# Edge messages of a four-layer graph network: moving one scaled part per pair of tiles from ScalarE and TensorE to VectorE

## What is computed

```python
w = ssp(edge_attr @ W_f1) @ W_f2 * (ssp(s0 @ W_s1) @ W_s2)
w1, w2, w3, w4 = jnp.split(w, 4, axis=-1)
x0e, x1e = split_irreps(x[edge_src])
sh0, sh1 = (edge_sh[:, 0], edge_sh[:, 1:4])
out0 = w1 * x0e * sh0[:, None] + w4 * (jnp.einsum('eum,em->eu', x1e, sh1) / jnp.sqrt(3.0))
out1 = w2[:, :, None] * x0e[:, :, None] * sh1[:, None, :] + w3[:, :, None] * x1e * sh0[:, None, None]
edge_feat = merge_irreps(out0, out1)
out = jax.ops.segment_sum(edge_feat, edge_dst, num_segments=old_x.shape[0])
```

## Time and profile before

| | |
|---|---|
| median of 3 runs | 1556.94 us (1551.32 to 1558.68) |
| the profiled execution | 1552.31 us, with a span of 1550.4 us |
| busy share of the span | PE 89%, DVE 74%, ACT 50%, POOL 47% |
| `interaction_edges` within the span | its steady steps lie between about 900 and 1360 us |
| granted TensorE clock there | 1.00 of full speed |

### The profile page before, as it was taken

The page is one execution under the profiler, slowest core; times in us unless marked ns, Lnnn a source line. Parts: engine busy times, 40 slices in busy tenths (PEclk is TensorE's granted clock), DMA queues, the critical chain, the costliest instruction groups (busy, mean ns, idle before and its releaser), DMA issues. The chain is left out here.

```text
span 1550.4 us, 22449 instructions
## 1 busy us (share of the span) xinstructions
PE 1379.4 (89%) x6771; PEld 820.1 (53%) x6771; DVE 1145.0 (74%) x2024; ACT 779.7 (50%) x1997; POOL 733.9 (47%) x768
## 2 busy tenths in 40 slices
PE   5589899899997939999957599999999999985998
PEld 3245577644444539989855344444444444443443
DVE  8977588641206578999936599999999999996023
ACT  2155355300000238979734188878787878761100
POOL 0000399537750357100004588888888888840000
PEclk9889999999998858979878799999999999997999
DMA  8994000000001020500011544444444444401001
GB/s 234 51 113 153 1 2 2 1 8 16 15 11 40 8 113 16 81 1 1 1 37 41 186 140 143 153 152 144 144 150 154 143 147 146 150 25 36 26 14 41
DMA packets 96964, 117.81 MB, mean 76 GB/s; under 512 B 50065, under 2 KB 78225, under 8 KB 96849
## 3 DMA queue, kind: packets, MB, share of 16 engines
q1 hardware_dynamic: 80497, 44.83, 16.5%
q0 software_dynamic: 16352, 71.55, 14.9%
HBM read 96.02 MB, written 11.55 MB: 69 GB/s over the span
## 5 line engine op out<-in xcount | busy, mean ns | idle before, releaser
L431 POOL TENSOR_SCALAR hot_i<-iota_row,il 128x128 f32<-128x128 bf16 x125 | 108.1, 881 | 178.8 <-DVE il L453 172.0
L1426 POOL DMA_INDIRECT far<-far_rows,far_node x150 | 167.6, 1118 | 43.9 <-issue 26.6
L613 POOL DMA_INDIRECT records<-recs,place_i x136 | 137.1, 1008 | 87.4 <-issue 40.9
L1041 PE MATMUL sum_ps<-wx,prob_t 128*128 128x65 f32 x1024 | 140.2, 297 | 12.2 <-DVE prob_t L1073 12.2
L1041 PEld LDWEIGHTS sum_ps<-wx,prob_t 128*128 128x128 f32 x1024 | 138.2, 217 | 13.9 <-DVE prob_t L1073 13.9
L1574 ACT ACTIVATE far<-far,recs 128x128 f32<-128x128 f32 x450 | 138.6, 386 | 0.0
L367 PE MATMUL perm_ps<-hot_high,hot_low 128*128 128x400 f32 x272 | 97.3, 521 | 21.4 <-ACT hot_high L237 21.4
L708 PE MATMUL gcn_ps<-pair,hs 128*128 128x512 f32 x256 | 112.0, 600 | 3.2 <-DVE hs L771 3.2
L1471 PE MATMUL near_ps<-near_parts,hot_t 128*128 x450 | 89.0, 335 | 10.4 <-DVE hot_t L1603 10.4
L1563 ACT ACTIVATE pair<-f_ps,recs 128x256 f32<-128x256 f32 x150 | 72.0, 480 | 51.7 <-PE s_ps L1507 51.7
L777 DVE SCALAR_TENSOR_TENSOR h<-gcn_out_ps,root_p,bias_gcn 128x512 f32<-128x512 f32 x16 | 12.0, 752 | 116.0 <-PE gcn_out_ps L718 116.0
(11 more groups left out here) (332 smaller groups left out, 3272.8 us busy)
## 6 DMA issues: line engine op xcount, KB each, us to landing
pair<-zeros SPq DMA_DIRECT2D x1, 8576.0 KB, 58.5
places<-local_rows SPq DMA_DIRECT2D x75, 64.0 KB, 3.9
s_all<-s_rows SPq DMA_DIRECT2D x8, 512.0 KB, 7.8
records<-empty_record SPq DMA_DIRECT2D x1, 2925.0 KB, 70.7
far<-far_rows,far_node POOLq DMA_INDIRECT x150, 4.7
recs<-in_edge_attr SPq DMA_DIRECT2D x1, 2176.0 KB, 26.8
records<-recs,place_i POOLq DMA_INDIRECT x136, 2.2
w_gcn<-in_L_gnn_W_gcn SPq DMA_DIRECT2D x2, 1024.0 KB, 7.4
```

Of the source, the lines that this page charges most:

```text
L431: nc.gpsimd.tensor_scalar(hot_i[:, g % 2, k, 1, :], c.iota_row[:], il[:, t + k:t + k + 1], None, ALU.is_equal).then_inc(hot_i_ready, 1)
L613: c.nc.gpsimd.indirect_dma_start(c.rows[:, :], bass.IndirectOffsetOnAxis(ap=c.place_i[:, t:t + 1], axis=0), c.recs[:, t, :], None).then_in ...
L1041: last = nc.tensor.matmul(sum_ps[b % 2][:, h // 4, at:at + DH + 1], prob_t[:, n % PS, k, :], wx[:, k, h, :], start=(k == 0), stop=(k == NB ...
L1426: nc.gpsimd.indirect_dma_start(far[:, u % UNROLL, k, :], None, c.far[:, :], bass.IndirectOffsetOnAxis(ap=far_node[:, t:t + 1], axis=0)) \
```

## The change

The table `BY_ACT` says which vector parts ScalarE makes, for the first and for the second tile of a group. For the first tile it held parts 0 and 1, and now holds part 0 alone, as for the second tile. `BY_DVE` is what is left over.

```diff
-    BY_ACT = ((0, 1), (0,))
+    BY_ACT = ((0,), (0,))
     BY_DVE = tuple(tuple(m for m in range(3) if m not in taken) for taken in BY_ACT)
```

## The result

The changed kernel is slower. Its median is 1568.99 us (1567.19 to 1572.66, 4 runs), against 1555.80 us (4 runs) before. The ratio is 1.0097, with a 95% interval of 1.0074 to 1.0121. The prediction said 1561, between 1553 and 1577, and put its highest chance (0.60) on no change that can be measured. The time is inside the range, 8 us above the value, and in the class with 0.30. Between the medians before and after lie 13.2 us, where the prediction added up 4.3.

The account below looks back on a forecast made before the run. TensorE was taken as the bound at 6.72 us, the VectorE and GpSimd loop second at 6.51, rising to 6.775. The terms 3.6 + 0.3 + 0.8 - 0.4 gave +4.3 us, so 1561 us, range 1553 to 1577.

Parts of the forecast that it names:

- What bounds the kernel now: Steady steps: TensorE's own work sets the 6.72 us period; the loop of VectorE and GpSimd is second at 6.51.
- TensorE's 0.22 and ScalarE's instruction are lost: L1518 gets 0.22 us shorter and ScalarE drops about 0.33 us; neither shortens the period, as TensorE will wait.
- The loop takes over: Closed loop through VectorE and GpSimd goes from 6.51 to 6.775 us and sets the period; forecast, chance 0.70.
- its price is the distance of starts: VectorE's fourth L1663 costs the distance between pass starts, 0.263 us, not its duration.
- The forecast's own band: Whole kernel: 1559 to 1564 us from pass price, slack and ends; 1555 to 1568 with the scatter of the runs.
- a rival in which the slack of 0.21 is not free: GpSimd's wait for L1525 costs 0.21 anyway, so the whole 0.26 shows: 1577 us; chance 0.22 together with the port rival.
- The class "slower": Measurably slower whole kernel: chance 0.30, being 0.22 from the two slower rivals plus 0.08 from scatter.
- The other price: Fourth pass on VectorE by the skill page's latency rule: 0.194 us, loop 6.70, sum about -1 us.
- The slack of 0.21: Loop of VectorE and GpSimd has 0.21 to 0.22 us to spare per step before GpSimd's L1455.
- The rival at the port: VectorE's fourth pass pushes L1667 into GpSimd's copy L1434 at the shared port: 1580 us; chance 0.22 with the slack rival.
- The sum with 0.263: Whole kernel with the pass at 0.263 us: period 6.775, +4.3 us in all, +0.3%.
- The longer path at 6.62: Two-period path from L1625 through TensorE, L1525, L1455 and L1650 to a later L1625: 6.62 us a period, not binding.

Follow-up runs that it names:

- e2: Kernel before with only TensorE's half of the change: L1518 has 256 columns instead of 384, one term left out; 1540.65 us.
- e8: Changed kernel with one more VectorE pass per group ahead of L1650, written to an unread slot; 1569.67 us, period 6.908.
- e1: Kernel before with only VectorE's half of the change: one more fused pass per group, written to an unread slot; 1568.18 us, period 6.908.
- e11: Changed kernel with GpSimd's copy L1434 ahead of its two gathers; the period falls by 0.048 us.
- e9: Changed kernel with L1667 between the third and the fourth fused pass; 1561.48 us, ratio 1.0035.
- e10: Kernel of e9 with one L1611 moved behind L1603 as well; 1550.02 us, ratio 0.9976.
- e12: Kernel of e10 with L1518 at 128 columns instead of 256, one term left out; 1548.33 us, ratio 0.9963.
- e7: Changed kernel with only the second of the two L1611 moved behind L1603; ratio 1.0003, period 6.711.
- e3: Changed kernel with both L1611 moved behind L1603; 1576.42 us.
- e5: Changed kernel with a fifth fused VectorE pass; ScalarE keeps part 0 of the first tile only, L1523 has 128 columns; 1588.82 us.
- e6: Changed kernel with L1667 ahead of the four fused passes; 1587.16 us.
- e4: Kernel before with both L1611 moved behind L1603; slower by 1%, steps of 6.79 and 7.12 us alternate.

## Why the prediction was right or wrong

*What bounds the kernel now: right.* TensorE's own work set 6.72, and the loop of L1455, L1650, the passes, L1603 and L1444 stood at 6.51. e2 runs at 6.519 with nothing but 128 columns of L1518 taken away. VectorE's 49.7 of 50 us was no bound: e8 puts 0.26 us more into its queue at no cost.

*TensorE's 0.22 and ScalarE's instruction are lost: right.* e1 has neither and runs at the changed kernel's period.

*The loop takes over, at 6.51 plus the price of a pass: right. The price: wrong.* The step that failed is the term "its price is the distance of starts", 0.263. The fourth pass costs 0.363 at the place where it lands, and the first L1611 0.04 more, so the loop is 6.908 and not 6.775. Over 69 steady steps that is 9.2 us, and it accounts for the 8.9 between the forecast's rise of 4.3 and the 13.2 measured. The rest of the sum held about: for the first step and the last ones 1.1 us were forecast, and the trace has 0.4 in the first and 0.7 in the last four. The prediction also named a growing row of L1663 among the signs that it is wrong. That row grew, from 0.34 to 0.44 us.

*The range: right by its allowance.* The forecast's own band ended at 1564, and at 1568 with the scatter of the runs. The 1569 is inside the range because its top, 1577, was drawn for a rival in which the slack of 0.21 is not free. That rival did not come true. The class "slower" had its 0.30 from that rival, from the meeting at the port with the copy and from scatter, and from none of what happened. The place in the range is luck. The other price that the prediction worked out, 0.194, is seen at no pass: none costs under 0.26.

*The slack of 0.21: right.* Had there been none, the period would have been 6.72 + 0.40.

*The rival at the port: wrong in its form.* The gather stayed at 0.96, the copy L1434 at 0.27, and L1667 at 0.41. The cost fell on the pass, beside a gather that itself showed nothing, and by e11 it goes with GpSimd's order. The prediction looked at what would meet the copy and not at what would stand beside the gather.

*The sum with 0.263:* e9 takes the extra away by order alone, and has the period 6.772 and the ratio 1.0035, against 6.775 and +0.3% in the prediction.

*The longer path at 6.62: right, and out of sight in the changed kernel.* In e10 it is the bound at 6.626, and in e12 it gives way to 6.575.

What stays open: why a fused pass is 0.10 longer when it starts about 0.31 us behind the start of the second gather, and L1667, with twice the elements, is not. e11 ties it to GpSimd's order, in which the second gather is what runs beside the pass; what the gather does at that moment no run shows. Single steps say a little more. In one step of e7 the gather starts 0.05 later and in one of e3 0.10 later, and the fourth pass costs 0.26 in both. But in one step of e1 (its L1455 starts at 1247.71) it costs 0.26 with the gather where it always is, so the distance from the gather's start isn't the whole condition. The 0.04 on L1611 appears where it starts 0.04 behind the copy and is missing where it doesn't (e5, e6); in e3 L1603 starts there, and it pays the 0.04 instead. It wasn't tried by itself.

## What to carry to other kernels

Look for the loop that comes second, and for the slack in front of the bound: 0.2 us a step decided here that 0.22 us less on TensorE bought nothing, because the same edit put 0.4 us into the loop behind it. An instruction much longer than its size, with an end at a fixed distance behind another engine's instruction, contains a wait; work ahead of it is free, and work between it and the next signal is not. Take the price of an added instruction from a row at the place where it will stand, and ask what the other engine does there.

## What the runs showed of the hardware

A single-input VectorE instruction of 128x128 f32 in SBUF (L1611) was held for 0.55 us by a GpSimd add (e3). Which of the two is held turned on some hundredths of recorded start: up to 0.018 us ahead of the add L1611 always lost, from 0.022 ahead it always won and the add took 0.84 us instead of 0.73, and between them both are seen (e3, e4). A VectorE pass of 128x128 with two inputs cost 0.36 us instead of 0.26 beside one stretch of GpSimd's indirect gather, in all steady steps but single ones, and the extra shrank to 0.03 when the copy was put ahead of the gathers and the second one started 0.41 us later (e11).
